# Loads of x and stores of the output divided over more partitions, and one-hot matrices with the slot innermost, in a graph layer on one core

## What is computed

```python
xn = layernorm(x)
h = relu(xn @ W1 + b1); w = sigmoid(h @ W2 + b2)          # one gate per node
num = segment_sum(xn[dst] * w[dst], src); den = segment_sum(w[dst], src)
x = x + where(den > 0, num / max(den, 1e-12), 0) + mix(xn)  # mix: 8 heads, k^T v over all nodes, times q, plus xn
x = x + ffn(layernorm(x))    # router (256->128->6), top 2 of 6 experts, each 256->256->256->256 with biases b1, b2, b3
```

## Time and profile before

| | us |
|---|---|
| median of 3 runs (2786.73 to 2791.58) | 2786.89 |
| the profiled execution | 2783.34 |
| its span in the profile | 2781.6 |

### The profile page before, as it was taken

The page is one execution under the profiler, slowest core; times in us unless marked ns, Lnnn a source line. Parts: engine busy times, 40 slices in busy tenths (PEclk is TensorE's granted clock), DMA queues, the critical chain, the costliest instruction groups (busy, mean ns, idle before and its releaser), DMA issues.

```text
span 2781.6 us, 53408 instructions
## 1 busy us (share of the span) xinstructions
PE 2196.4 (79%) x18096; PEld 1961.3 (71%) x18096; DVE 1760.5 (63%) x4212; ACT 1157.1 (42%) x2861; POOL 494.1 (18%) x414
## 2 busy tenths in 40 slices
PE   0002477654499999999999999999999999999997
PEld 0001366644388888888888888888888888888886
DVE  4203489899686666566666666666666666666662
ACT  0001234324444544444444454544445445444444
POOL 0001967778710000000000000000000000000000
PEclk9999677757699999999999999999999999999999
DMA  1000000001120000000000000000000000000000
GB/s 44 27 29 23 0 0 1 1 10 46 52 72 5 5 5 6 5 4 6 5 4 6 5 4 5 6 5 4 6 5 4 6 5 4 5 6 4 4 5 7
DMA packets 29005, 30.83 MB, mean 11 GB/s; under 512 B 7283, under 2 KB 26852, under 8 KB 28703
## 3 DMA queue, kind: packets, MB, share of 16 engines
q1 hardware_dynamic: 25758, 26.97, 2.9%
q0 software_dynamic: 3200, 3.28, 0.4%
HBM read 16.55 MB, written 13.70 MB: 11 GB/s over the span
## 4 chain that ended last, share of the span: by engine, by line
PE 55%; DMA 12%; issue 9%; POOL 8%; DVE 7%; another core or an unknown queue 7%; DVEq 1%; ACT 0%; SPq 0%; POOLq 0%; ACTq 0%
PE turned L1148 24%; DMA out_rows<-feat_mem 12%; PE front L1182 9%; PE front L1190 8%; PE front L1173 7%; PE turned L1130 4%; POOL acc_mem L639 4%; DVE sort_mem L1399 2%; DVE sort_mem L1475 2%; POOL tab_mem L625 1%; POOL sort_mem L701 1%; DVE feat_mem L1593 1%; PE front L1216 1%; DVE feat_mem L1586 1%
## 5 line engine op out<-in xcount | busy, mean ns | idle before, releaser
L1475 DVE TENSOR_TENSOR sort_mem<-lane_bf,sort_mem 128x512 bf16<-128x512 bf16 (+1 forms) x1372 | 829.5, 646 | 188.1 <-PE turned L1130 176.4
L1148 PE MATMUL turned<-acc_mem,sort_mem 128*128 128x257 bf16 x4998 | 707.7, 278 | 0.5 <-ACT sort_mem L935 0.5
L927 ACT ACTIVATE sort_mem<-turned 128x512 bf16<-128x512 f32 (+2 forms) x686 | 371.9, 542 | 486.7 <-PE turned L1130 486.6
L1148 PEld LDWEIGHTS turned<-acc_mem,sort_mem 128*128 128x128 bf16 x4998 | 486.3, 100 | 84.0 <-issue 0.5
L887 ACT ACTIVATE feat_mem<-front,b 128x128 f32<-128x128 f32 x1176 | 366.3, 363 | 380.2 <-PE front L1173 201.1
L715 POOL DMA_INDIRECT sort_mem<-kept_keys,key_at x100 | 110.4, 1104 | 1807.4 <-DVE key_at L1433 1791.7
L1399 DVE TENSOR_TENSOR sort_mem<-sort_mem 128x320 f32<-128x320 f32 (+2 forms) x568 | 345.7, 671 | 3.0
L1182 PE MATMUL front<-feat_mem 128*128 128x128 f32 x2352 | 337.9, 289 | 1.1 <-ACT feat_mem L887 1.1
L1130 PE MATMUL turned<-sort_mem 128*128 128x128 bf16 (+1 forms) x2695 | 247.4, 213 | 100.1 <-DVE sort_mem L1475 100.1
L1173 PE MATMUL front<-feat_mem 128*128 128x128 f32 x2352 | 322.4, 280 | 1.4 <-ACT feat_mem L887 1.4
L1182 PEld LDWEIGHTS front<-feat_mem 128*128 128x128 f32 x2352 | 298.9, 199 | 18.8 <-issue 15.6
(11 more groups left out here) (217 smaller groups left out, 2358.0 us busy)
## 6 DMA issues: line engine op xcount, KB each, us to landing
gated_rows<-tab_mem SPq DMA_DIRECT2D x49, 128.5 KB, 2.3
out_rows<-feat_mem SPq DMA_DIRECT2D x49, 127.0 KB
feat_mem<-in_L_ffn_expert_w SPq DMA_DIRECT2D x18, 256.0 KB, 5.9
base<-in_x SPq DMA_DIRECT2D x1, 3556.0 KB
base<-in_x SPq DMA_DIRECT2D x1, 2667.0 KB
sort_mem<-kept_keys,key_at POOLq DMA_INDIRECT x100, 2.6
kept_keys<-sort_mem SPq DMA_DIRECT2D x1, 832.0 KB, 4.4
gath_mem<-in_src SPq DMA_DIRECT2D x1, 781.2 KB
```

The costliest lines, as they stand in the source:

```text
L927: nc.scalar.activation(a_tiles[:, k % 2, :, :].rearrange("p s n -> p (s n)")[:, 0:width], ps_a[k % 2][:, 0:width], ACT.Copy).then_inc(S["a ...
L1148: last = nc.tensor.matmul(ps_agg, a_tiles[:, k % 2, n, :], y_part(t, part), start=(t == 0 and part == 0), stop=(t == BLOCKS - 1 and part = ...
L1475: nc.vector.tensor_tensor(hot[:, k % 2, 0:count, 0:lanes], lane_bf[:, 0:lanes].unsqueeze(1).broadcast_to([P, count, lanes]), edge_tab[:, a ...
```

## The change

- Lanes 0 to 126 are no longer one DMA: x is loaded in lanes 0 to 111, 112 to 126 and 127, three DMAs for each part. The output blocks 0 to 26 are stored by one DMA of all 128 lanes, the blocks 27 to 48 by two, of 112 and 15 lanes.
- The one-hot rings are laid out (ring, lane, slot), slot innermost. `lane_bf` holds each lane number four times in a row, 128 x 4. L1475 reads it as it lies, reads `edge_tab` as a row of four that is repeated for every lane, and writes one dense run. The last group now marks four slots too. TensorE reads slot n of the ring with a step of four elements, both as weights and as the moving operand.
- `b3` moves into the memory of the features that are dead by then, and is loaded behind the 18 expert weights; its waits move with it.

```diff
+LANE_PARTS = (slice(0, 112), slice(112, LANES))
...
-        hot_dst, hot_src, a_tiles = (ring(A_GROUP * P) for _ in range(3))
+        hot_dst, hot_src = (ring(A_GROUP * P).rearrange("p r s n -> p r (s n)").rearrange("p r (n s) -> p r n s", s=A_GROUP) for _ in range(2))
+        a_tiles = ring(A_GROUP * P)
...
+        b3 = after(DIM)[0:EXPERTS, :]
...
-        lane_bf = sb("lane_bf", [P, P], BF16)
+        lane_bf = sb("lane_bf", [P, P, A_GROUP], BF16)
...
-            sp.dma_start(base[0:LANES, at:to, :], node_rows[0][:, at:to, :]).then_inc(x_loaded[0], 16)
-            sp.dma_start(base[LANES:P, at:to, :], last_rows[0][:, at:to, :]).then_inc(x_loaded[0], 16)
+            def load_rows(part, at, to):
+                for lanes in LANE_PARTS:
+                    sp.dma_start(base[lanes, at:to, :], node_rows[lanes, at:to, :]).then_inc(x_loaded[part], 16)
+                sp.dma_start(base[LANES:P, at:min(to, SHORT), :], last_rows[:, at:min(to, SHORT), :]).then_inc(x_loaded[part], 16)
+
+            load_rows(0, at, to)
             sp.wait_ge(S["x_zeroed"], 1)
-            sp.dma_start(base[0:LANES, rest_at:rest_to, :], node_rows[0][:, rest_at:rest_to, :]).then_inc(x_loaded[1], 16)
-            sp.dma_start(base[LANES:P, rest_at:SHORT, :], last_rows[0][:, rest_at:SHORT, :]).then_inc(x_loaded[1], 16)
+            load_rows(1, rest_at, rest_to)
...
+            sp.dma_start(b3, a["L0_ffn_expert_b3"]).then_inc(S["weights_loaded"], 16)
...
                 with sp.Fori(0, SHORT) as b:
                     sp.wait_ge(S["ey_added"], 1 + EXPERTS * (first + b + 1))
-                    sp.dma_start(node_rows[1][:, bass.ds(b, 1), :], y_acc[0:LANES, :].unsqueeze(1)).then_inc(S["row_stored"], 16)
-                    sp.dma_start(last_rows[1][:, bass.ds(b, 1), :], y_acc[LANES:P, :].unsqueeze(1)).then_inc(S["row_stored"], 16)
+                    sp.dma_start(out[bass.ds(b, P, BLOCKS), :], y_acc).then_inc(S["row_stored"], 16)
+                    sp.nop().then_inc(S["row_stored"], 16)
                 with sp.Fori(SHORT, BLOCKS) as b:
                     sp.wait_ge(S["ey_added"], 1 + EXPERTS * (first + b + 1))
-                    sp.dma_start(node_rows[1][:, bass.ds(b, 1), :], y_acc[0:LANES, :].unsqueeze(1)).then_inc(S["row_stored"], 16)
-                    sp.nop().then_inc(S["row_stored"], 16)
+                    for lanes in LANE_PARTS:
+                        rows = bass.ds(b + lanes.start * BLOCKS, lanes.stop - lanes.start, BLOCKS)
+                        sp.dma_start(out[rows, :], y_acc[lanes, :]).then_inc(S["row_stored"], 16)
...
-            nc.gpsimd.iota(lane_bf[:, :], pattern=[[1, P]], base=0, channel_multiplier=0,
+            nc.gpsimd.iota(lane_bf[:, :, :], pattern=[[1, P], [0, A_GROUP]], base=0, channel_multiplier=0,
...
-                    last = nc.tensor.matmul(ps_a[k % 2][:, at:at + width], hot_dst[:, k % 2, n, :], hot_src[:, k % 2, n, 0:width],
+                    last = nc.tensor.matmul(ps_a[k % 2][:, at:at + width], hot_dst[:, k % 2, :, n], hot_src[:, k % 2, 0:width, n],
                                             start=True, stop=True)
...
-            pe.wait_ge(S["weights_loaded"], 16 * 3 * EXPERTS)
+            pe.wait_ge(S["weights_loaded"], 16 * (3 * EXPERTS + 1))
...
                 for hot, at, lanes in ((hot_dst, SLOT_ROWS, P), (hot_src, 0, width)):
                     at += slots_here[0]
-                    nc.vector.tensor_tensor(hot[:, k % 2, 0:count, 0:lanes], lane_bf[:, 0:lanes].unsqueeze(1).broadcast_to([P, count, lanes]),
-                                            edge_tab[:, at:at + count].unsqueeze(2).broadcast_to([P, count, lanes]),
+                    nc.vector.tensor_tensor(hot[:, k % 2, 0:lanes, :], lane_bf[:, 0:lanes, :],
+                                            edge_tab[:, at:at + A_GROUP].unsqueeze(1).broadcast_to([P, lanes, A_GROUP]),
                                             ALU.is_equal).then_inc(S["hot_ready"], 1)
```

More of the change, by code:

```diff
@@ L341, in gps_layer @@
         b1, b2 = sb("b1", [P, EXPERTS, HALVES]), sb("b2", [P, EXPERTS, HALVES])
-        b3 = sb("b3", [EXPERTS, DIM])
         bound = sb("bound", [P, BLOCKS + 1], I32)
@@ L447, in gps_layer @@
         SPREAD_LINKS = 3
-        N_SMALL = 13
+        N_SMALL = 12
         N_MIX_LOADS = 6
@@ L478, in gps_layer @@
         assert ordered.shape == keys[1].shape
-        node_rows = [t[0:LANES * BLOCKS, :].rearrange("(p t) d -> p t d", t=BLOCKS) for t in (a["x"], out)]
-        last_rows = [t[LANES * BLOCKS:NODES, :].unsqueeze(0) for t in (a["x"], out)]
+        node_rows = a["x"][0:LANES * BLOCKS, :].rearrange("(p t) d -> p t d", t=BLOCKS)
+        last_rows = a["x"][LANES * BLOCKS:NODES, :].unsqueeze(0)
         kept_chunks = kept_keys[0:COLS, :].rearrange("(t p) q -> p t q", p=P)
@@ L507, in _ @@
             sp.dma_start(router_b2[:, :], a["L0_ffn_router_b2"].rearrange("(o e) -> o e", o=1)).then_inc(S["small_loaded"], 16)
-            sp.dma_start(b3[:, :], a["L0_ffn_expert_b3"]).then_inc(S["small_loaded"], 16)
             with nc.allow_non_contiguous_dma(reason="biases and head weights with the feature on the partition, once"):
@@ L763, in _ @@
             act.wait_ge(S["small_loaded"], 16 * N_SMALL)
-            act.wait_ge(x_loaded[0], 32)
+            act.wait_ge(x_loaded[0], 48)
             act.wait_ge(S["x_norm"], 1)
@@ L813, in _ @@
                 front_round(u)
-            act.wait_ge(x_loaded[1], 32)
+            act.wait_ge(x_loaded[1], 48)
             act.wait_ge(S["x_norm"], 2)
@@ L1363, in statistics @@
                 at, to = X_PARTS[part]
-                dve.wait_ge(x_loaded[part], 32)
+                dve.wait_ge(x_loaded[part], 48)
                 dve.wait_ge(S["x_zeroed"], 1)
@@ L1470, in mark_group @@
                 slots_here = slots_of_group(k)
-                count, width = len(slots_here), place_of_slot(slots_here[0])[2]
+                width = place_of_slot(slots_here[0])[2]
                 dve.wait_ge(S["built"], g + 1)
```

## The result

The changed kernel takes 2578.35 us (median of 4 runs, 2576.85 to 2583.17) where the kernel before takes 2786.81 (4 runs beside it): a ratio of 0.925, 95% interval 0.9235 to 0.9267. That is 208 us or 7.5% less; the forecast was 333 us less. The profiled execution has a span of 2575.1 us, 206.5 less than the 2781.6 of before. Of all executions in this document one is left out of its median: one of the four of the second experiment took 9961.3 us, where the other three took 2830.5 to 2834.4.

What follows compares the result with a forecast made beforehand. Three stages bound it: the load of x, then sort and small work, then a TensorE loop with a hole each round from the output store. 197.6 + 126 + 6 + 3 = 333 us less: 2454 us, own range 2435 to 2475, 8-in-10 2415 to 2560.

Steps and rivals of the forecast that it cites:

- Reads with a step of four: TensorE's builds from the one-hot matrices in the loop: strided reads cost 0, within bounds of 0 to +144 us.
- rival 2: TensorE's builds in the loop: strided reads at half rate, +144 us, 2598 us, or 2475 to 2598 in part; chance 0.15.
- the weights' side might suffer alone: TensorE's builds: if only the weights' reads slow down, the kernel takes 2475 to 2598 us.
- the front: Everything before the 47-round loop: forecast to move earlier by the whole 197.6 us wait for x.
- x loads: Start of kernel: VectorE's whole wait for x goes, 197.6 us gained, with 7 us of waiting possibly staying.
- L631 keeps its 35 us: GpSimd's 28-column multiply before the loop (L625 before the change) still takes 35 us beside VectorE's sort.
- Stores: Output stores land in the gated rows' 2.3 us, not 7.0; TensorE's hole goes: 126 us in loop, 6 at end.
- Rival 4: Split transfers run as slowly as before, the x wait stays, 27 of 49 blocks gain: about 2705 us; chance 0.03.
- Marks: VectorE's one-hot marks at L1475: up to 0.26 us faster each, worth nothing in the loop, 3 us elsewhere.
- Front gains or loses by L625: Before the loop, GpSimd's multiply L625: up to 33 us more gained, or 7 to 20 us lost.
- rivals 1 and 5: Before the loop: 1, L625 let through, 33 us more, 2421, chance 0.12; 5, 7 to 20 lost, within forecast's chance.
- the sign that I had named for these rivals: Before the loop: a GpSimd L625 of another length would show that the front gains or loses by it.

Runs made afterwards that it cites:

- the second experiment: The new one-hot layout alone (with b3's load moved) on the kernel before, loads and stores left in one piece: 2833.5 us, ratio 1.016.
- the two single experiments: On the kernel before, the loads of x alone split: 2601.3 us, ratio 0.932; the stores of the output alone split: 2647.1 us, ratio 0.948.

## Why the prediction was wrong

The step that failed is "**Reads with a step of four** ... I take 0", out of 0 to 144 us. I argued that only the addresses change; they are what counts. Measured: 115 to 118 ns a build instead of 55, and 121 us in all. The term's upper end was near this in size, 119 ns by the f32 row, but by luck: its reason, each element a read of its own, would make a step of eight cost the same, and that took 232 ns. Of the 144 us, 121 arrive because the matmuls behind the builds give some back. The sum with it at 144, rival 2, gave 2598; the changed kernel took 2578.4. It had 0.15, and the range ended at 2560. The remark that the weights' side might suffer alone was the wrong way round: that side pays nothing. The sum with this term at 0 gave 2454 us, and the kernel without the step took 2457.8. That these agree so well is in part luck too, since by the two single experiments the front was 15 us too high and the stores 9 too low.

I let the rule of the Trainium skill weigh in here ("Advanced Engine Details and Errata", section "Memory Cachelines"), which asks for at least two hits on each 16-byte line; a step of four bf16 gives two. The runs contradict it for TensorE's moving operand: two hits a line cost double (0.47 us for four builds), one hit four times (0.93), and only with four hits was the step free (0.23).

The other steps, in the order of the prediction:

- **x loads**, 197.6 us: 183 by the loads alone. The waits went in full; 11 us came back because I took the edges' 15.4 us as safe, being ahead in the queue. The other 4 are within what the first marks differ by between kernels with the same loads. Being issued first did not keep them first once x occupied all engines. That x lands at 24 and 35 us at 337 GB/s was too good too: stretches of 5 us moved 143 to 249 GB/s from 10 to 35 us. Nothing hung on it, since VectorE came for x at 51 and 66. That L631 keeps its 35 us held: 35.03.
- **Stores**, 126 + 6: the stores alone took 136.7 us off the span while the first marks came 4.0 later, so 140.7. Right in mechanism (no hole, clock 1.00), 9 us short: the undisturbed round is 37.98, not 38.15, 45 x 0.17 = 8 us. Rival 4 is out: the split stores land in 1.7 and 1.5 us, sooner than the 2.3 I took from the gated rows. The Trainium skill's advice against splitting over partitions ("DMA: Bandwidth & Descriptors", section "Rules for kernel authors") does not fit a count like 127, where one piece took 7.0 us and two take 1.7 and 1.5; the same page's rule on how many engines a DMA gets (one for 127 partitions, 16 for 112) agrees with the shares of the DMA engines' time in the stretches, 0.06 and 1.09.
- **Marks**, 3 us: their speed was as forecast (419 ns), and worth no more than that; TensorE's waits for them are 6.2 us with slow marks, 2.2 with quick ones.
- **Front gains or loses by L625** (rivals 1 and 5): neither in the changed kernel, where the long one, now L631, started at 83.29 us, the 72.6 forecast and 11 for the edges. In two kernels (weights alone, step of two) the 28-column L631 took 0.25 us but came at 123 us instead of 83, behind an L627 of 41 us; the part's last GpSimd instruction came at 123.6 and 123.9 us instead of 118.4, and the first marks at 575 and 568, like those of the others. So a multiply of another length, the sign that I had named for these rivals, does not tell them: the pause had moved to another GpSimd instruction. Which of them it meets, and why, was not tried.

The account of the change: 188.5 us in front, some 140 by the stores, less 121 for the reads and the rest within a few us: 206.5.

## What to carry to other kernels

A layout that makes one engine's operation faster is to be priced at every reader, and first at the reader that sets the end: here VectorE, which had time to spare, gained 0.26 us a mark, and TensorE, which had none, paid some 60 ns a build. If an unknown has two ends and the bound engine executes it thousands of times with no slack, "no row shows it" argues for the dear end as much as for zero; and a layout in between (here pairs) may have both. When a load is made wide, look at who shares the engines with it, also at what was issued before it.

## What the runs showed that I had not expected

- TensorE's moving operand in bf16: a step of 2 elements free (57 ns for 128 columns), 4 elements 115 to 118 ns, 8 elements 232 ns. The weights' load: 97 ns without a step, 114 with a step of four on the weights alone, at no cost; 145 with eight on both operands, where the build itself takes 232.
- A load issued first (edges, 0.8 and 1.2 us) landed at 26.3 us instead of 15.4, because a wider load was issued 0.3 us behind it on the same queue. Why the earlier descriptors do not keep their place on the shared engines stays open.
- One GpSimd instruction on 28 columns takes 35 to 41 us beside VectorE's sort in every kernel here, the multiply L631 (L625 before) in most, L627 in two; the same multiply on the first part's 21 columns takes 1.54.
